# Fetching the last 13 edge columns of two segmented sums row by row from SyncE and ScalarE

## The reference, cut to what matters

```
# third layer (2 edge types): the message is a function of (type, source)
agg = segment_sum(where(rel == r, edge_nn(h[src], W_rel[r], b_rel[r])), dst)
# fourth layer (8 edge types)
msg = einsum('nd,rde->rne', h, weight)[edge_type, src]
m   = segment_sum(msg, dst);   out = h @ sl_w.T + sl_b + m / max(deg, 1)
```

## Time and profile before

| | us |
|---|---|
| median of three runs | 5032.83 |
| the profiled execution | 5049.07 |
| its span, first to last instruction | 5047.3 |
| sweep of `rel`, first to last gather issue | 3680.3 to 4176.5 |
| sweep of `typ`, first to last gather issue | 4500.9 to 4997.9 |
| GpSimd busy over the span | 3280.7 |
| VectorE busy over the span | 3042.4 |

### The profile page before, as it was taken

How to read it: one execution, slowest core, us unless ns; L and a number is a source line. 1 busy time by engine, 2 the same in 40 slices (tenths; PEclk the granted TensorE clock), 3 DMA queues, 4 the chain that set the end, 5 groups by cost and what they waited for, 6 DMA issues and landing times.

```text
span 5047.3 us, 62489 instructions
## 1 busy us (share of the span) xinstructions
PE 2975.9 (59%) x15472; PEld 2145.7 (43%) x15472; DVE 3042.4 (60%) x9095; ACT 1009.0 (20%) x2805; POOL 3280.7 (65%) x3289
## 2 busy tenths in 40 slices
PE   3121288767888688878888788888800006962100
PEld 2011176655776565556555565555700003431000
DVE  6754256656666688877877778887533331224433
ACT  1000010001000243335333353333500003420000
POOL 4767667775777477774777747776067772027776
PEclk7555599998999899999999999999955557985555
DMA  5656566665666443333333333333166662246665
GB/s 178 197 169 217 190 192 209 207 209 164 208 211 210 134 124 103 104 103 95 102 103 104 103 93 103 105 104 88 58 213 207 208 207 90 92 147 204 206 207 188
DMA packets 279688, 776.83 MB, mean 154 GB/s; under 512 B 64561, under 2 KB 103474, under 8 KB 275506
## 3 DMA queue, kind: packets, MB, share of 16 engines
q0 software_dynamic: 157104, 429.21, 30.7%
q1 hardware_dynamic: 122242, 343.62, 17.8%
HBM read 455.64 MB, written 316.93 MB: 153 GB/s over the span
## 4 chain that ended last, share of the span: by engine, by line
PE 25%; POOL 13%; DMA 11%; issue 8%; DVE 5%; ACT 1%; DVEq 1%; POOLq 0%; ACTq 0%; SPq 0%
POOL HC L497 11%; PE PS L1263 8%; PE PS L1255 5%; DMA X<-table,idx_src 3%; PE PS L1189 3%; DMA HC<-table,idx_src 3%; PE PS L952 3%; DMA HC<-table_typ,run_typ 3%; DMA HC<-table_rel,run_rel 2%; POOL HC L473 1%; DVE work L1896 1%; PE PS L1244 1%; POOL X L473 1%; PE PS L1151 1%; PE PS L946 1%
## 5 line engine op out<-in xcount | busy, mean ns | idle before, releaser
L1711 DVE SCALAR_TENSOR_TENSOR HC<-HC,run_rst 128x256 f32<-128x256 f32 x1890 | 915.2, 484 | 1156.1 <-DMA HC<-table,run_max 496.6
L497 POOL DMA_INDIRECT HC<-table,run_max x1113 | 1145.8, 1029 | 445.6 <-issue 308.8
L473 POOL DMA_INDIRECT HC<-table,idx_src x648 | 644.5, 995 | 355.1 <-DMA table<-B 158.5
L1059 PE MATMUL PS<-AM,ring 128*128 128x256 f32 x3000 | 710.7, 392 | 142.0 <-DVE ring L1694 141.3
L473 POOL DMA_INDIRECT X<-table,idx_src x600 | 604.3, 1007 | 182.9 <-issue 130.8
L1059 PEld LDWEIGHTS PS<-AM,ring 128*128 128x128 f32 x3000 | 569.8, 194 | 279.3 <-DVE ring L1694 202.4
L1255 PE MATMUL PS<-AM,work 128*128 x3744 | 650.8, 285 | 27.9 <-DVE score L1896 26.8
L1952 DVE SCALAR_TENSOR_TENSOR HC<-HC,fcol,PS 128x257 f32 x1248 | 586.1, 470 | 104.5 <-PE PS L1263 93.5
L497 POOL DMA_INDIRECT HC<-table_typ,run_typ x391 | 379.0, 969 | 398.0 <-DMA table_typ<-HC 279.1
L1093 PE MATMUL PS<-ident,HC 128*128 128x128 f32 x10 | 3.4, 444 | 1001.1 <-DVE HC L1711 1001.1
L497 POOL DMA_INDIRECT HC<-table_rel,run_rel x391 | 378.3, 967 | 287.3 <-DMA table_rel<-AM 168.4
(11 more groups left out here) (259 smaller groups left out, 4197.9 us busy)
## 6 DMA issues: line engine op xcount, KB each, us to landing
prefix<-HC SPq DMA_DIRECT2D x485, 512.0 KB, 3.2
table_typ<-HC SPq DMA_DIRECT2D x19, 1024.0 KB, 3.8
HC<-table,run_max POOLq DMA_INDIRECT x1113, 3.9
HC<-table,idx_src POOLq DMA_INDIRECT x648, 2.8
table<-AM SPq DMA_DIRECT2D x15, 640.0 KB, 3.7
table<-B SPq DMA_DIRECT2D x15, 640.0 KB, 3.3
X<-table,idx_src POOLq DMA_INDIRECT x600, 2.8
table_rel<-AM SPq DMA_DIRECT2D x10, 640.0 KB, 4.1
```

The costliest lines, as they stand in the source:

```text
L473: pool.indirect_dma_start(held(t)[:, 0:D], None, table, bass.IndirectOffsetOnAxis(ap=idx_src[:, t:t + 1], axis=0)).then_inc(landed[t % AHE ...
L497: pool.indirect_dma_start(run_slot(k), None, src, bass.IndirectOffsetOnAxis(ap=run_idx[s[1]][:, j:j + 1], axis=0)).then_inc(landed[k], 16)
L1059: last = nc.tensor.matmul(PS[:, (2, 5)[c % 2], 0:D], quads[:, (QUADS * x + g) % 4, b % 4, :], A[:, b, :], start=(b == 0), stop=(b == BLOCK ...
L1711: V.scalar_tensor_tensor(run_slot(k), run_slot((j - 1) % SLOTS), run_rst[:, j:j + 1], fresh, fade, join).then_inc(pooled, 1)
```

## The change

In `rel` and `typ` GpSimd's loop skips the columns from 378 on (`swept(s)`), so it gathers 378 of 391. The other 13 are read as single rows of 1 KB by plain DMAs with a source address from a register: columns 378 to 383 (768 rows) by SP, columns 384 to 390 (896 rows) by ScalarE, into a region of the tile AM that has one place per column. For this an input `singles` brings source indices and types in row order; SP loads them, VectorE turns them into table rows on one partition (`one_src`, 1,664 numbers) and releases both issuers by `singles_known`. `fetch` loads 32 indices into registers and then issues 32 DMAs. ScalarE issues its rows in one piece; SP issues up to nine ahead of each turn's store, from the second turn on. VectorE's steps of columns 378 to 390 wait for `x_in` of their column group instead of `landed`, and for `written` of the slot. The ring `far_src` of the maxima has three places instead of four, which frees memory. The core of the diff:

```diff
--- before.py
+++ after.py
@@ -34,6 +34,9 @@
 SLOTS = 24
 TEAMS = SLOTS // 4
 TURNS = -(-TILES // 4)
+BY_SP, BY_ACT = 6, 7
+SINGLES = BY_SP + BY_ACT
+BITE = 32
 PICKED = list(range(37, TILES - 5, 12))
 QUADS = -(-BLOCKS // 4)
 SPAD = 512
...
@@ -175,7 +178,7 @@
 
         run_idx = {n: sb(f"run_{n}", [P, TILES], I32) for n in ("max", "rel", "typ")}
         node_id = sb("node_id", [P, BLOCKS])
-        far_src = sb("far_src", [P, 4, P], I32)
+        far_src = sb("far_src", [P, 3, P], I32)
         run_rst = sb("run_rst", [P, TILES])
         span_rst = sb("span_rst", [P, P])
         end_at = sb("end_at", [P, BLOCKS], I32)
@@ -233,6 +236,28 @@
         def run_slot(k):
 
             return flatC[:, k * D:(k + 1) * D]
+
+        def swept(s):
+
+            return TILES if s[1] == "max" else TILES - SINGLES
+
+        def single(j):
+
+            return AM[:, (j - TILES + SINGLES) * D:(j - TILES + SINGLES + 1) * D]
+
+        def single_sem(j):
+
+            return x_in[(j - TILES + SINGLES) // 3 if j < TILES - BY_ACT else 2 + (j - TILES + BY_ACT) // 4]
+
+        def singles_in(n, j):
+
+            k, rounds = (j - TILES + SINGLES) // 3 if j < TILES - BY_ACT else 2 + (j - TILES + BY_ACT) // 4, before(n, ("runs",)) - 2
+            return 16 * (2 + rounds * P * (3, 3, 4, 3)[k])
+
+        one_at = 4096
+        one_src = AM[0:1, one_at:one_at + SINGLES * P].bitcast(I32)
+        one_type = AM[0:1, one_at + SINGLES * P:one_at + 2 * SINGLES * P].bitcast(I32)
+        one_f = AM[0:1, one_at + 2 * SINGLES * P:one_at + 3 * SINGLES * P]
 
         def halves(v):
             return v.rearrange("p (c e) -> p c e", c=K2)
...
@@ -390,7 +416,7 @@
 
         def columns(s, k, upto=TILES):
 
-            return sum(1 for j in range(k, upto, SLOTS) if j not in picked_in(s)) if k < SLOTS else 0
+            return sum(1 for j in range(k, min(upto, swept(s)), SLOTS) if j not in picked_in(s)) if k < SLOTS else 0
 
         def picks_before(n):
 
...
@@ -429,6 +455,21 @@
         def part(b, a):
 
             return G[:, bass.ds(b, 1), a, :].rearrange("p o d -> p (o d)")
+
+        def fetch(eng, rows, first, j, p, count):
+
+            regs = nc.values_load_multi_w_load_instructions(
+                one_src[0:1, bass.ds(first, count)], engines=(eng.engine,), min_val=0, max_val=rows.shape[0] - 1,
+                skip_runtime_bounds_check_because="the indices are the graph's own")[1]
+            for i in range(count):
+                eng.dma_start(single(j)[p + i:p + i + 1, :], rows[bass.ds(regs[i], 1), :]).then_inc(single_sem(j), 16)
+                yield
+
+        def fetch_all(eng, rows, first_j, columns_of):
+
+            for j in range(first_j, first_j + columns_of):
+                for p in range(0, P, BITE):
+                    yield from fetch(eng, rows, (j - TILES + SINGLES) * P + p, j, p, BITE)
 
         def block_regs(eng, s, count=RING):
 
@@ -492,7 +533,7 @@
 
                             pool.wait_ge(written[g % TEAMS], 16 * (drained(n, g % TEAMS) + g // TEAMS))
                             pool.wait_ge(pooled, m * TILES + j - SLOTS + 5)
-                        if j in picked_in(s):
+                        if j in picked_in(s) or j >= swept(s):
                             continue
                         pool.indirect_dma_start(
                             run_slot(k), None, src,
@@ -570,11 +611,27 @@
                         load_row("slb", 1)
                     grid = prefix[0:TILES * P].rearrange("(p j) d -> p j d", j=TILES)
                     far = 0
+                    one_by_one = iter(())
+                    if s[1] != "max":
+                        if s[1] == "typ":
+                            for k in range(WIDES):
+                                sp.wait_ge(wided[k], 16 * len(range(k, BLOCKS, WIDES)))
+                        else:
+                            sp.wait_ge(rel_tabled[0], 16 * REL2 * 3)
+                            sp.wait_ge(rel_tabled[1], 16 * REL2 * 2)
+                        sp.dma_start(one_src, singles[0:1, :]).then_inc(loaded, 16)
+                        sp.dma_start(one_type, singles[1 if s[1] == "rel" else 2:2 if s[1] == "rel" else 3, :]).then_inc(loaded, 16)
+                        one_by_one = fetch_all(sp, table_rel if s[1] == "rel" else table_typ, TILES - SINGLES, BY_SP)
                     for g in range(TURNS):
+                        if s[1] != "max" and g >= 1:
+                            if g == 1:
+                                sp.wait_ge(singles_known, 1 if s[1] == "rel" else 2)
+                            for _ in range(9):
+                                next(one_by_one, None)
                         while far < len(picked_in(s)) and picked_in(s)[far] // 4 - 10 <= g:
-                            if far >= 4:
-                                sp.wait_ge(quad_made, QUADS * (picks_before(n) + far - 3))
-                            sp.dma_start(far_src[:, far % 4, :], picks[far:far + 1, :].to_broadcast([P, P])).then_inc(far_in[far % 4], 16)
+                            if far >= 3:
+                                sp.wait_ge(quad_made, QUADS * (picks_before(n) + far - 2))
+                            sp.dma_start(far_src[:, far % 3, :], picks[far:far + 1, :].to_broadcast([P, P])).then_inc(far_in[far % 3], 16)
                             far += 1
                         size = min(4, TILES - 4 * g)
                         if m == 0 and g == 29:
@@ -840,6 +897,9 @@
                     act.sem_inc(stage_done, 1)
                 elif s == ("runs", "rel"):
                     begin(act, n)
+                    act.wait_ge(singles_known, 1)
+                    for _ in fetch_all(act, table_rel, TILES - BY_ACT, BY_ACT):
+                        pass
                     funcs = (("i", ACT.Sigmoid), ("g", ACT.Tanh), ("o", ACT.Sigmoid))
 
                     def take_ends(b):
@@ -934,6 +994,11 @@
                                     cell(q + 2)
                     act.wait_ge(wide_out, 4 * BLOCKS)
                     act.sem_inc(stage_done, 1)
+                elif s == ("runs", "typ"):
+                    begin(act, n)
+                    act.wait_ge(singles_known, 2)
+                    for _ in fetch_all(act, table_typ, TILES - BY_ACT, BY_ACT):
+                        pass
 
 
         @block.tensor
...
@@ -1689,11 +1754,18 @@
                                     else:
                                         dve.wait_ge(quad_used, (z - 4) // QUADS * (QUADS - 1) + (z - 4) % QUADS + 1)
                                 size = min(4, BLOCKS - 4 * g)
-                                src = far_src[:, c % 4, :].rearrange("p (o e) -> p o e", o=1).to_broadcast([P, size, P])
+                                src = far_src[:, c % 3, :].rearrange("p (o e) -> p o e", o=1).to_broadcast([P, size, P])
                                 at = node_id[:, 4 * g:4 * g + size].rearrange("p (k o) -> p k o", o=1).to_broadcast([P, size, P])
                                 V.tensor_tensor(quads[:, z % 4, 0:size, :], src, at, ALU.is_equal).then_inc(quad_made, 1)
                                 yield
 
+                    if not most:
+                        dve.wait_ge(loaded, 16 * (8 if s[1] == "rel" else 10))
+                        if s[1] == "rel":
+                            link(V.scalar_tensor_tensor(one_f, one_type, float(NODES), one_src, ALU.mult, ALU.add))
+                        else:
+                            link(V.scalar_tensor_tensor(one_f, one_src, float(REL8), one_type, ALU.mult, ALU.add))
+                        V.tensor_copy(one_src, one_f).then_inc(singles_known, 1)
                     work_inside, quads_inside = inside(), make_quads()
                     for j in range(TILES):
                         k = j % SLOTS
@@ -1701,6 +1773,11 @@
                         if j in picked_in(s):
                             dve.wait_ge(picked, picks_before(n) + PICKED.index(j) + 1)
                             fresh = PS[:, (2, 5)[PICKED.index(j) % 2], 0:D]
+                        elif j >= swept(s):
+                            q = j // 4 % TEAMS
+                            dve.wait_ge(written[q], 16 * (drained(n, q) + j // 4 // TEAMS))
+                            dve.wait_ge(single_sem(j), singles_in(n, j))
+                            fresh = single(j)
                         else:
                             dve.wait_ge(landed[k], 16 * (landings(n, k) + columns(s, k, j + 1)))
                             fresh = run_slot(k)
@@ -2040,6 +2117,13 @@
     return np.ascontiguousarray(rows[2][:, PICKED].T)
 
 
+def single_rows(rows):
+
+    import numpy as np
+
+    return np.ascontiguousarray(rows[2:5, :, TILES - SINGLES:].transpose(0, 2, 1).reshape(3, SINGLES * P))
+
+
 def kernel(**inputs):
     import numpy as np
     import concourse.bacc as bacc
```

(12 more changed lines are left out.)

## The result

The changed kernel took 5024.66 us, median of 20 runs (5019.46 to 5032.63), beside 5033.49 us for the kernel before on the same chips (20 runs, 5024.53 to 5044.79). The ratio is 0.9984, with a 95% interval of 0.9977 to 0.9990: 8 us faster, between 5 and 12, inside the 0.3% that the prediction counted as no change. The forecast was 19 us. The profiled execution has a span of 5018.3 us, against 5047.3 before. That difference isn't the gain: 13.0 of the 29.0 us stand ahead of `rel`'s first gather (3667.3 against 3680.3), a time that varies by as much between kernels that are alike up to there.

A forecast was written before the change was run, and what follows sets the result against it. GpSimd's issue time per column was taken as the bound. Two sweeps at 9.5 us gain 19: 5049.1 - 19 = 5030 us profiled, 5014 us for the median, which stands 0.32% lower; range for 8 in 10: 5006 to 5139.

The forecast's parts named there:

- (a): Rival, VectorE's step of column 388: ScalarE's rows come late at 0.57 to 0.65 us each, costing 52 to 195 us; chance 0.30.
- (b): Rival, SP and ScalarE issuing together: they share something, up to 0.94 us per row on ScalarE, costing 717 us; chance 0.10.
- (c): Rival, ScalarE's row fetches: 0.53 to 0.55 us per row, just at the edge, within 15 us of before; chance 0.08.
- (d): Rival, end of the sweeps: stores at 3.45 us per turn bind, gain 13 us; counted as lower half of the forecast's 0.52.
- The price of a row: ScalarE's and SP's issue time per fetched row: 0.50 us taken, bounded by 0.43 and 0.65.
- The point from which the change is worth nothing: ScalarE's rows against the end of the sweep: at 0.541 us per row the gain is gone.
- SP's 18 us of slack: SP's stores behind its row fetches: they may fall 18 us behind before GpSimd is held, only above about 0.55 us per row.
- GpSimd loses 13 gathers per sweep: End of each sweep: column 377 is last, 13 VectorE steps of 0.588 us follow; 9.5 us gained per sweep, 19 for both.
- up to 1 us: Landing of the last store at the end of a sweep: up to 1 us of the gain may be lost, counted as nothing.
- the 9.5 between 9.0 and 9.9: Gain per sweep at its end: 9.9 us with column 377's lag of 2.8, 9.0 with column 390's 3.7; 9.5 taken.
- The same bytes, so DMA load stays at 0.65: DMA engines in the sweeps: 1,664 KB of rows replace 13 gathers of 128 KB, so their load stays at 0.65.
- keeps up: SP's queue: nine rows and a store take 4.9 us of a 5.09 us turn, so it holds up to 0.525 us per row.

## Why the prediction was right, and where not

**The direction, the mechanism and the range held; the forecast gain was more than double the measured one.** 5014 was forecast, 5024.7 came, inside 5006 to 5139 and outside the forecast's own 5006 to 5022. Rivals (a) and (b) didn't come. (c) named a time within 15 us of before, and that came, but not its reason, a row price at the edge. (d) named a gain of 13, the very number of the sweeps, but its reason, stores every 3.45 us at the end, isn't there: the last stores are issued 2.47 us apart, each full one lands 2.6 us behind its issue, and the last is issued at 4160.70, as its step ends. That the number fits is luck.

*Right.* The price of a row, 0.50, measured 0.496 and 0.489; ScalarE was done 27 us early, where 22 was written. That column 377 is last, and the 13 steps behind it run without a wait. The point from which the change is worth nothing, which eight columns on ScalarE bore out. SP's 18 us of slack, which the spread columns bore out. `far_src`, and the issuers sharing next to none of their issue time.

*The price was right by chance in its parts.* I took the issue at 0.47 from two DMAs that follow each other; one-row DMAs go at 0.370 with their address operation. I took the load at 0.035 per row, the low end; 0.08 came, above even the high end of 0.069, which was worked out from 16 registers. The two errors cancel.

*The step whose size failed: "GpSimd loses 13 gathers per sweep", by four terms that it counted at nothing or a little short.* Of the forecast 19 us, 13.2 are in the sweeps of the trace:

- GpSimd's pace was taken as unchanged. It went from 1.272 to 1.277 and from 1.274 to 1.280, 3.8 us over both sweeps. The kernel without rows is back at 1.274 and 1.273. It isn't the rows as such: the five sweeps in which SP issues nine rows a turn beside ScalarE's, without waits for stores, have 1.277 to 1.281, and the fourteen others without such waits 1.262 to 1.275, among them those with twelve spread columns. The median instruction is within 3 ns of before; 49 and 62 of the change's gathers take over 1 us, 42 and 46 before, 47 and 50 without rows. What makes them long, no run shows.
- 13 steps at 0.618, not 0.588, 0.8 us over both. With the rows and VectorE's wait for them gone, it was 0.589. ScalarE's last row was issued at 4129.0, 24 us before the first of these steps, so the wait instruction is the likelier cause.
- L504 starts 4.0 us behind the start of the last step, where it was 3.5 before. That is 0.9 us over both. It isn't the "up to 1 us" of the last store that I named and counted at nothing: the last store, of three columns, lands 2.30 us behind its issue before and 2.29 in the change (the 3.45 of the earlier trace rows is the store ahead of it). The time lies in GpSimd's own semaphore instructions. Before, the last of them (L503) was already waiting, from 4174.49 to 4183.09. In the change six come behind the landing at 4162.99, one every 0.087 us:

```profile
L543 POOLq EVENT_SEMAPHORE  x5: 43/43/43, 4163.0 to 4163.4; - x5
L544 POOLq EVENT_SEMAPHORE  x1: 43/43/43, 4163.4 to 4163.4; - x1
```

  The kernel without rows has the six and the 4.0 too; the one with twelve spread columns has the form of before, and 3.5.
- Column 377 is added 3.5 us behind its issue in `rel` and 3.1 in `typ`; it was 2.8 before, and the 9.5 between 9.0 and 9.9 stands for 3.2. That is 0.3 more and 0.1 less, 0.2 over both; without rows it was 2.7 and 2.8.

These make 5.7 where 5.8 are missing. Each is small, but the forecast gain was itself only 9.5 us of a sweep of 504, and every term that I counted at nothing lay on the same side.

*"The same bytes, so DMA load stays at 0.65."* True of the mean (0.67) and wrong of the one engine that carries the rows. At the change's rate it costs at least a part of the last term above, and no run shows how much of the others; at a rate 14% higher (4.3 against 3.8 rows per us) it costs more than the whole gain. The register loads, which I had treated as a mere price, keep the stream slow enough. I had taken it from the windows view that no DMA engine is full, which a mean can't show. The Trainium skill (DMA: Bandwidth & Descriptors, "Rules for kernel authors") wants many small transfers coalesced, since under 64 KB they are mostly overhead. I had read this as the issuer's time and as a reason for the high end, 0.65, where 0.496 came; the runs show the cost of the small transfers at the one engine.

*SP "keeps up".* I expected no lag. In `rel` the stores stood 7.5 to 10.8 us behind VectorE's step until SP's rows were issued, because SP started 20.2 us into the sweep and nine rows with a store take a whole turn, 9 x 0.564 = 5.08 us against 4 x 1.277 = 5.11, so it never caught up. In `typ` it was 0 to 3.8. It cost nothing, the slack being 18. The start was nearly as forecast, since the indices took 2.9 us and not 4.0:

```profile
3679.53 1.88 DVE L1765 SCALAR_TENSOR_TENSOR AM<-AM 1x1664 f32<-1x1664 int32 x1 [17.64 <-DMA AM<-singles]
3681.45 1.01 DVE L1768 CAST AM<-AM 1x1664 int32<-1x1664 f32 x1
```

*What stays open.* The sweeps are 13.2 us shorter in the trace, the runs 8 with 5 to 12. In the table most variants show 3 to 7 us more in the sweeps than in the runs. I looked for the difference in the other stretches of the fourteen traces: from L504 to `typ`'s first gather it is 314 to 319 us in all, the end behind the second L504 42 us (45 in one), and the start of `rel` lies anywhere from 3667 to 3680 us, whatever the kernel. With one trace of before, and a scatter of that size ahead of the sweeps, the remaining 5 us can't be placed. It may be that its sweeps were a little long in that one execution: the kernel with three places in `far_src`, whose sweeps are those of before, has 1.9 us less in them. There is no second trace of before.

## What to carry to other kernels

When work is taken off the engine that sets the pace, look at where in its order the removed pieces stood: at the end of a serial chain they leave a tail of the next engine's steps, in mid-chain they don't, and the same fetches then brought 19 to 24 us instead of 8. Many DMAs of one piece must be counted against one DMA engine and not against the mean share of sixteen; the last of a transfer's sixteen increments shows it. And a queue that also issues what others wait for (here the stores) needs room per turn: eight rows left it 6 us behind at most, nine up to 20.6.

## What I had not expected of the hardware

- A load of 32 registers took 2.15 to 3.48 us on ScalarE, where 16 on TensorE's queue took 1.106: about 0.07 us per register, and a little more beside the row traffic.
- A one-row DMA of 1 KB costs the issuer 0.213 us on ScalarE and 0.228 on SP, less than the smallest shape of before, 0.302; in four separate pieces 0.584.
- A single-row DMA is the work of one DMA engine, and by the increments those of both issuers go to the same one of sixteen. Beside gathers and stores at a mean share of 0.65 it keeps up with 3.8 rows per us and not with 4.3: a gather's landing goes from 2.85 to 4.0 and 8.0 us, a store's from 3.8 at the first rate to 17.6 at the second (where the rows read are also always the same).
- GpSimd's pace is 1.262 to 1.281 us per column in sweeps that wait for no store, with a median instruction of 0.946 to 0.949 us in all, and lowest with SP's rows alone; it goes by how many gathers take over 1 us, 21 to 62 per sweep.
- Waits are instructions too: six semaphore instructions of GpSimd behind the last landing put its next gather off by 0.5 us.
